# Experts' first norm moved from ScalarE to VectorE, row scaling from VectorE to GpSimd, and a quad's stages in eight slots instead of eleven

## The reference, cut to what matters

```python
def _moe(y):                       # for each row the expert idx = argmax(y @ Wg.T)
    h = relu(y @ W1[e] + b1[e])    # 128 -> 512
    return h @ W2[e] + b2[e]       # 512 -> 128
y = _layer_norm(x + _mha(x), g1, be1)
z = _layer_norm(y + _moe(y), g2, be2)    # times g2, plus be2
x = x + _layernorm(z)                    # a second norm, no weights, plus the residual
```

## Time and profile before

| what | value |
|---|---|
| median of the runs | 1222.24 us (1218.07 to 1223.42) |
| span of the profiled execution | 1168.2 us |
| its own device time | not listed apart; 54.0 us lie between its span and the median |
| PE busy over the span | 1051.2 us (90%) |
| DVE, ACT, POOL busy | 1032.2, 1008.1, 897.8 us |
| experts alone on TensorE | from about 1033 to 1138 us of the span |
| after TensorE's last matmul | about 30 us |

### The profile page before, as it was taken

How to read it: one execution, slowest core, us unless ns; L and a number is a source line. 1 busy time by engine, 2 the same in 40 slices (tenths; PEclk the granted TensorE clock), 3 DMA queues, 4 the chain that set the end, 5 groups by cost and what they waited for, 6 DMA issues and landing times. The chain is left out here.

```text
span 1168.2 us, 25817 instructions
## 1 busy us (share of the span) xinstructions
PE 1051.2 (90%) x8346; PEld 883.1 (76%) x8346; DVE 1032.2 (88%) x1971; ACT 1008.1 (86%) x2143; POOL 897.8 (77%) x648
## 2 busy tenths in 40 slices
PE   7699999899999999999999999879888877999990
PEld 3488887788878888788787887867565555999990
DVE  6999999899999999999999999998589987677773
ACT  3989999899999999999999999986589985678882
POOL 2499999799999999999899998978226666445455
PEclk9899999999999999999999999999899998999995
DMA  7634333243334333334334233343376656886640
GB/s 198 195 110 119 99 120 104 98 124 94 120 97 120 122 102 117 114 100 125 99 121 126 92 106 96 109 145 105 79 172 168 163 141 194 271 245 236 230 160 27
DMA packets 151746, 156.57 MB, mean 134 GB/s; under 512 B 47136, under 2 KB 97058, under 8 KB 151614
## 3 DMA queue, kind: packets, MB, share of 16 engines
q1 hardware_dynamic: 146270, 142.30, 41.3%
q0 software_dynamic: 5344, 12.63, 3.0%
HBM read 111.42 MB, written 23.20 MB: 115 GB/s over the span
## 5 line engine op out<-in xcount | busy, mean ns | idle before, releaser
L1169 POOL TENSOR_TENSOR cm<-rows_or_blocks 128x1024 f32<-128x1024 f32 x256 | 604.0, 2371 | 77.5 <-DVE rows_or_blocks L982 75.9
L982 DVE TENSOR_TENSOR_SCAN rows_or_blocks<-abuf,hstate,bank_pair 128x512 f32<-128x512 f32 x512 | 612.2, 1260 | 16.2 <-PE bank_pair L511 6.1
L534 PE MATMUL bank_pair<-ident,cm 128*128 128x128 f32 x2048 | 252.6, 273 | 1.2 <-POOL cm L1169 1.2
L534 PEld LDWEIGHTS bank_pair<-ident,cm 128*128 128x128 f32 x2048 | 229.7, 141 | 10.7 <-issue 8.5
L778 ACT ACTIVATE abuf<-xg_or_delta,aneg 128x512 f32<-128x512 f32 x256 | 166.6, 712 | 4.2 <-DVE rows_or_blocks L982 3.4
L778 ACT ACTIVATE abuf<-delta,aneg 128x512 f32<-128x512 f32 x256 | 166.4, 713 | 4.3 <-DVE rows_or_blocks L982 4.3
L514 PE MATMUL bank_pair<-ident,ub 128*128 128x128 f32 x1024 | 135.2, 274 | 12.4 <-ACT ub L789 6.9
L514 PEld LDWEIGHTS bank_pair<-ident,ub 128*128 128x128 f32 x1024 | 117.0, 142 | 30.9 <-issue 20.5
L429 PE MATMUL bank_pair<-xnT,rows_or_blocks 128*128 128x512 f32 x256 | 124.2, 601 | 5.1 <-DVE xnT L955 3.1
L2446 POOL DMA_INDIRECT out<-res,tokens x71 | 73.5, 1035 | 65.9 <-DVE res L2417 45.3
L789 ACT ACTIVATE ub<-vs_or_uT,bT 128x256 f32<-128x256 f32 x256 | 108.6, 497 | 0.2
(11 more groups left out here) (300 smaller groups left out, 1957.1 us busy)
## 6 DMA issues: line engine op xcount, KB each, us to landing
rows_or_blocks<-c_rows SPq DMA_DIRECT2D x256, 256.0 KB, 3.2
w_of_tile<-w SPq DMA_DIRECT2D x71, 256.0 KB, 2.7
rows_or_blocks<-routed SPq DMA_DIRECT2D x71, 128.5 KB, 2.4
xT_and_rstd<-in_xt SPq DMA_DIRECT2D x16, 257.5 KB, 3.6
xres<-in_x SPq DMA_DIRECT2D x16, 256.0 KB, 3.9
x_rows<-x1t SPq DMA_DIRECT2D x16, 256.0 KB, 3.7
xg_or_delta<-x_rows SPq DMA_DIRECT2D x16, 256.0 KB
v_rows<-vs_or_uT SPq DMA_DIRECT2D x16, 256.0 KB
```

Of the source, the lines that this page charges most:

```text
L534: mm = pe.matmul(ps_y[j // 2][:, (j % 2 * CH + c) * P:(j % 2 * CH + c + 1) * P], cm[:, n % CM_RING, c, j * P:(j + 1) * P], ident[:, :], is ...
L982: dve.tensor_tensor_scan(hbuf[:, n % RING, c, :], abuf[:, n % RING, c, :], ps_bx[n % 2 * CH + c][:, :], hstate[:, bass.ds(g * (NST * CH) + ...
L1169: pool.tensor_tensor(cm[:, n % CM_RING, :, :], hbuf[:, n % RING, :, :], c, ALU.mult).then_inc(s_cm, 1)
```

## The change

`norm_a` on ScalarE, the shift for it, and the pair of whole-quad operations `affine` go. In their place VectorE does two three-operand operations a tile: `centre_and_weigh` (slot 7), sum less mean times g2, and `scale_and_shift` (slot 8), times the reciprocal root plus be2. `scale_rows` goes to GpSimd, in slot 3, behind the scatters of the quad three before and ahead of the next scatters; it waits until `add_rows` of the quad before is done. `stats_b` is in slot 9 (was 11), its root in 10 (was 12), its shift in 11 (was 13), `norm_b` in 11 and 12 (was 14, 15), `add_x1` and `scatter` in 13 (was 16). `zn` is gone and `rows_and_expert` has one buffer.

```diff
-    ROOT_STEPS = 3
+    ROOT_STEPS = (2, 3)
+    STATS = (3, 2)
...
-    summed = sb("rows_and_expert", [P, 2, 4, D])
-    zn = sb("zn", [P, 2, 4, D])
+    summed = sb("rows_and_expert", [P, 4, D])
...
                 else:
-                    pe.wait_ge(S["stats_a"], 4 * (q - 2))
+                    pe.wait_ge(S["stats_a"], STATS[0] * (q - 3) + 1)
...
             for half in range(2):
-                for q in due(s, 14 + half):
+                for q in due(s, 11 + half):
                     norm_b(q, half)
-                for q in due(s, 8 + half):
-                    norm_a(q, half)
             for q in due(s, 7):
-                root(0, S["stats_a"], S["roots_a"], S["zn_ready"], q)
-            for q in due(s, 12):
+                root(0, S["stats_a"], S["roots_a"], S["z_ready"], q)
+            for q in due(s, 10):
                 root(1, S["stats_b"], S["roots_b"], S["z_out_ready"], q)
...
+        def centre_and_weigh(q):
+            dve.wait_ge(S["stats_a"], STATS[0] * (q + 1))
+            for i in range(tiles_of(q)):
+                b = dve.scalar_tensor_tensor(out=zg[:, i, :], in0=summed[:, i, :], scalar=mv_a[:, i, 0:1],
+                                             in1=w["rows"][:, 4, :], op0=ALU.subtract, op1=ALU.mult)
+            b.then_inc(S["zg_ready"], 1)
+
+        def scale_and_shift(q):
+            dve.wait_ge(S["roots_a"], ROOT_STEPS[0] * (q + 1))
             dve.wait_ge(S["zg_ready"], q + 1)
             if q >= 2:
                 dve.wait_ge(S["z_out_ready"], q - 1)
-            dve.tensor_tensor(z[:, q % 2, 0:n, :], zg[:, 0:n, :], row(5, n), ALU.add).then_inc(S["z_ready"], 1)
+            for i in range(tiles_of(q)):
+                b = dve.scalar_tensor_tensor(out=z[:, q % 2, i, :], in0=zg[:, i, :], scalar=rstd[0][:, i:i + 1],
+                                             in1=w["rows"][:, 5, :], op0=ALU.mult, op1=ALU.add)
+            b.then_inc(S["z_ready"], 1)
...
         def slot(s):
...
+            for q in due(s, 11):
+                less_mean(q)
             for q in due(s, 13):
-                less_mean(1, S["roots_b"], S["z_out_ready"], q)
+                add_x1(q)
             for q in due(s, 8):
-                less_mean(0, S["roots_a"], S["zn_ready"], q)
+                scale_and_shift(q)
             for q in due(s, 6):
                 add_rows(q)
                 stats_a(q)
-            for q in due(s, 5):
-                scale_rows(q)
-            for q in due(s, 16):
-                add_x1(q)
-            for q in due(s, 10):
-                affine(q)
-            for q in due(s, 11):
+            for q in due(s, 7):
+                centre_and_weigh(q)
+            for q in due(s, 9):
                 stats_b(q)
...
+        def scale_rows(q):
+            n = tiles_of(q)
+            if q == 0:
+                for i in range(4):
+                    pool.wait_ge(S[f"w1_loaded{i}"], 32)
+            else:
+                pool.wait_ge(s_rows[q % 4], 16 * sum(tiles_of(r) for r in range(q % 4 or 4, q + 1, 4)))
+                pool.wait_ge(S["stats_a"], STATS[0] * (q - 1) + 1)
+            pool.tensor_tensor(scaled[:, 0:n, :], rows[:, q % RINGS, 0:n, 0:D],
+                               w["rows"][:, 2, :].unsqueeze(1).broadcast_to([P, n, D]), ALU.mult)\
+                .then_inc(S["rows_scaled"], 1)
+
         def slot(s):
-            for q in due(s, 16):
+            for q in due(s, 3):
+                scale_rows(q)
+            for q in due(s, 13):
                 scatter(q)
```

More of the change, by code:

```diff
@@ L2132, in experts @@
     rstd = [sb(f"d_rstd_{c}", [P, 4]) for c in "ab"]
-    shift = [sb(f"d_shift_{c}", [P, 4]) for c in "ab"]
+    shift = sb("d_shift_b", [P, 4])
     names = """w1_loaded0 w1_loaded1 w1_loaded2 w1_loaded3 y_transposed yT_copied hidden_summed
-        hidden_ready expert_summed eps_set stats_a stats_b roots_a roots_b zn_ready zg_ready z_ready z_out_ready
+        hidden_ready expert_summed eps_set rows_scaled stats_a stats_b roots_a roots_b zg_ready z_ready z_out_ready
         res_ready out_scattered0 out_scattered1"""
@@ L2305, in root @@
             act.activation(rstd[n][:, :], (mv_a, mv_b)[n][:, :, 1], ACT.Ln, bias=eps[:, 0:1]).then_inc(s_out, 1)
-            act.wait_ge(s_out, ROOT_STEPS * q + 1)
+            act.wait_ge(s_out, ROOT_STEPS[n] * q + 1)
             act.activation(rstd[n][:, :], rstd[n][:, :], ACT.Exp, scale=-0.5).then_inc(s_out, 1)
-        def norm_a(q, half):
-            if half == 0:
-                act.wait_ge(S["roots_a"], ROOT_STEPS * (q + 1))
-                if q >= 2:
-                    act.wait_ge(S["zg_ready"], q - 1)
-            for i in range(2 * half, min(2 * half + 2, tiles_of(q))):
-                a = act.activation(zn[:, q % 2, i, :], summed[:, q % 2, i, :], ACT.Identity,
-                                   bias=shift[0][:, i:i + 1], scale=rstd[0][:, i:i + 1])
-            if half == 1:
-                a.then_inc(S["zn_ready"], 1)
         def norm_b(q, half):
             if half == 0:
-                act.wait_ge(S["roots_b"], ROOT_STEPS * (q + 1))
+                act.wait_ge(S["roots_b"], ROOT_STEPS[1] * (q + 1))
                 if q >= 2:
@@ L2326, in norm_b @@
                 a = act.activation(z_out[:, q % 2, i, :], z[:, q % 2, i, :], ACT.Identity,
-                                   bias=shift[1][:, i:i + 1], scale=rstd[1][:, i:i + 1])
+                                   bias=shift[:, i:i + 1], scale=rstd[1][:, i:i + 1])
             if half == 1:
@@ L2355, in stats @@
             if q >= 1:
-                dve.wait_ge(s_used, ROOT_STEPS * q)
+                dve.wait_ge(s_out, ROOT_STEPS[n] * q)
             for i in range(tiles_of(q)):
@@ L2359, in stats, with less_mean @@
             b.then_inc(s_bn, 1)
-        def less_mean(n, s_out, s_used, q):
-            dve.wait_ge(s_out, ROOT_STEPS * q + 2)
+        def less_mean(q):
+            dve.wait_ge(S["roots_b"], ROOT_STEPS[1] * q + 2)
             if q >= 1:
-                dve.wait_ge(s_used, q)
-            dve.scalar_tensor_tensor(out=shift[n][:, :], in0=(mv_a, mv_b)[n][:, :, 0], scalar=-1.0, in1=rstd[n][:, :],
-                                     op0=ALU.mult, op1=ALU.mult).then_inc(s_out, 1)
-        def scale_rows(q):
-            n = tiles_of(q)
-            if q == 0:
-                for i in range(4):
-                    dve.wait_ge(S[f"w1_loaded{i}"], 32)
-            else:
-                dve.wait_ge(s_rows[q % 4], 16 * sum(tiles_of(r) for r in range(q % 4 or 4, q + 1, 4)))
-                dve.wait_ge(S["stats_a"], 4 * q)
-            dve.tensor_tensor(scaled[:, 0:n, :], rows[:, q % RINGS, 0:n, 0:D],
-                              w["rows"][:, 2, :].unsqueeze(1).broadcast_to([P, n, D]), ALU.mult)\
-               .then_inc(S["stats_a"], 1)
+                dve.wait_ge(S["z_out_ready"], q)
+            dve.scalar_tensor_tensor(out=shift[:, :], in0=mv_b[:, :, 0], scalar=-1.0, in1=rstd[1][:, :],
+                                     op0=ALU.mult, op1=ALU.mult).then_inc(S["roots_b"], 1)
         def add_rows(q):
@@ L2382, in add_rows @@
             dve.wait_ge(S["expert_summed"], 4 * q + n)
-            dve.wait_ge(S["stats_a"], 4 * q + 1)
-            if q >= 2:
-                dve.wait_ge(S["zn_ready"], q - 1)
-            dve.tensor_tensor(summed[:, q % 2, 0:n, :], ps_f[q % 3][:, 0:n * D].rearrange("p (i d) -> p i d", i=n),
+            dve.wait_ge(S["rows_scaled"], q + 1)
+            dve.tensor_tensor(summed[:, 0:n, :], ps_f[q % 3][:, 0:n * D].rearrange("p (i d) -> p i d", i=n),
                               scaled[:, 0:n, :], ALU.add).then_inc(S["stats_a"], 1)
         def stats_a(q):
-            dve.wait_ge(S["stats_a"], 4 * q + 2)
-            stats(lambda i: summed[:, q % 2, i, :], stat_a, mv_a, S["stats_a"], 4 * q + 2, S["roots_a"], q)
-        def row(i, n):
-            return w["rows"][:, i, :].unsqueeze(1).broadcast_to([P, n, D])
-        def affine(q):
-            n = tiles_of(q)
-            dve.wait_ge(S["zn_ready"], q + 1)
-            if q >= 1:
-                dve.wait_ge(S["z_ready"], q)
-            dve.tensor_tensor(zg[:, 0:n, :], zn[:, q % 2, 0:n, :], row(4, n), ALU.mult).then_inc(S["zg_ready"], 1)
+            dve.wait_ge(S["stats_a"], STATS[0] * q + 1)
+            stats(lambda i: summed[:, i, :], stat_a, mv_a, S["stats_a"], STATS[0] * q + 1, S["roots_a"], 0, q)
+        def centre_and_weigh(q):
[6 more added lines that the diff above has]
+            dve.wait_ge(S["roots_a"], ROOT_STEPS[0] * (q + 1))
             dve.wait_ge(S["zg_ready"], q + 1)
```

6 lines of the change are left out of this document (3 added, 3 removed).

## The result

The changed kernel takes **1229.08 us** (median of 5 runs, 1227.20 to 1233.27); beside it the kernel before took 1218.07 (5 runs, 1215.90 to 1223.42). Ratio 1.0084, 95% interval 1.0057 to 1.0110: slower by 7 to 13 us. Forecast were 1218.1 us and a chance of 0.07 for slower. The forecast is wrong, and the time lies outside the range.

A forecast was written before the change was run, and what follows sets the result against it. TensorE was taken to bound the steady experts, and the delay to quad 15's result plus GpSimd's scatters the tail. Terms: 0 steady, -4.85 tail, +0.75 padding, together -4.1 us from 1222.24 to 1218.1 us; range 1213.5 to 1222.

The forecast's parts named there:

- My sum is made against the profiled span of 1168.2 us: Whole kernel: savings and costs were summed on one profile's 1168.2 us span, then put on the median of 1222.24 us.
- outside the span 54 us up to the median; both stay: Whole kernel: 54 us outside the span, and 8 us between the last scatter's issue and the span's end, stay unchanged.
- Cost in the steady stretch: 0.: Experts alone, 1033 to 1138 us: TensorE's 8.02 us a quad covers VectorE's new work and waits, so 0 us.
- ScalarE's relu and copy keep about 1 us in hand: Experts' steady stretch: ScalarE's relu and copy have about 1 us to spare before they would delay TensorE.
- Group 15 ... 13 us in hand, cost 0.: Attention's tail: group 15 scattered at about 1030.6 instead of 1021.8 us, wanted at 1043.74, so cost 0.
- padi ... +0.75 us.: Attention's tail: VectorE's padi comes at 1019.57 instead of 1018.82 us and delays TensorE through SyncE's queue by 0.75 us.
- The tail: 4.85 us earlier.: After TensorE's end: quad 15's scatters start 5.5 us earlier, and GpSimd's last scatter issue comes 4.85 us earlier.
- The pause behind them: Tail: GpSimd stands still for 1.1 us between quad 15's scatters and quad 16's, whose residual comes later.
- The new operations' price: VectorE's three-operand operations take 1.04 to 1.13 us for four, bounds 0.87 and 1.37; eight a quad.
- The rival with VectorE's period: Steady stretch: at 0.6 us per new operation VectorE's period becomes the bound, 1231 us; chance 0.06 including a combined case.
- VectorE and GpSimd stop each other: Experts: GpSimd's multiplication and VectorE's two-input SBUF operations exclude each other, tail 1.2 us later, 1219.3 us; chance 0.15.
- No row of this trace shows the case: Earlier trace: no row was said to show VectorE's two-input SBUF operation and GpSimd's operation excluding each other.

The follow-up runs named there:

- e14: Changed kernel with experts' and attention's routing scatters in pairs, and quad 1's two pairs moved to slots 20 and 21: 1179.18 us, ratio 0.9635.
- e6: Kernel before with one scatter a slot (16 to 19), each behind a further expert sum, still four in a row: 1227.3 us, ratio 1.0033.
- e7: Changed kernel with the experts' scatters one to a slot (13 to 16), so that they come in pairs: 1199.3 us, ratio 0.9804.
- e9: Kernel before with each quad's four experts' scatters in two pairs, the second two slots later: 1200.0 us, ratio 0.9787.
- e1: Kernel before, unchanged, timed and profiled again: 1224.0 us, ratio 0.9997, profiled span 1223.6 us.
- e13: Changed kernel with the four scatters of the experts' quad 1 moved to slot 20, behind the scaling for quad 4: 1227.5 us, ratio 1.0047.
- e2: Changed kernel with only the row scaling moved back from GpSimd to VectorE, in slot 5: 1233.3 us, ratio 1.0088.
- e12: Changed kernel with experts' and routing scatters in pairs, and quad 0's pairs moved to slots 16 and 17: 1181.5 us, ratio 0.9673.
- e10: Changed kernel with the experts' scatters in pairs and attention's routing scatters in two pairs too (slots 21 and 23): 1181.5 us, ratio 0.9660.

## Why the prediction was wrong, step by step

- **"My sum is made against the profiled span of 1168.2 us"; "outside the span 54 us up to the median; both stay."** This failed first. The 54 us lie inside it, and for the most part they were ScalarE's gaps and what they cost, in attention and in the experts: the changed kernel with its scatters in pairs runs 43.9 us under the kernel before (e14). A profile 4% shorter than every run of its kernel is of another course of events, and the rest of its rows tell of that one.
- **"Cost in the steady stretch: 0."** Measured: +6.0 us (1.7 to 8.5 over all profiles). The step that failed is "ScalarE's relu and copy keep about 1 us in hand", and that this covers everything. 1.3 us are in hand, but the relu comes 2.5 and 3.35 us late in the two quads shown, in a gap beside GpSimd's scatters that the prediction had no term for. The loss goes with the new slots; by what path is open, since the place of the scatters doesn't explain e6. Where the gaps are gone (e7 against e9) the step is right: 72.7 us both.
- **"Group 15 ... 13 us in hand, cost 0."** The delay came (6.5 us against e1; 8.8 forecast). Its cost did not come by the path that was looked at, SyncE's row loads, but by GpSimd's own queue: the delayed scatters joined the next four, and ScalarE stood still for 5.85 us and TensorE for 4.34. +5.4 us between tiles 16 and 28 (+5.7 from 12 on), of which 3.0 are back with the row broken (e13), most of them as faster busy time; 2.7 are open.
- **"padi ... +0.75 us."** Not to be seen; tile 16 starts 1.5 us earlier than in e1, no more than attention's own gaps vary.
- **"The tail: 4.85 us earlier."** Right, path and size: from the last outward group to the span's end 25.0 against 30.3, 5.3 us; 5.4 in e7 against e9. Quad 15's scatters start 3.5 us behind it and not 8.6: 5.1 us earlier (5.5 forecast). The pause behind them was 0.40 us and not 1.1.
- **The new operations' price**: four in 1.14 us (1138.43), forecast 1.04 to 1.13, bounds 0.87 and 1.37; in three groups 2.74 to 2.84 and in one 1.42, where GpSimd's multiplication runs beside them. GpSimd's multiplication 1.19, forecast 1.28.
- **The rival with VectorE's period** did not happen; it had the right sign and the wrong mechanism. Neither it nor any other rival asked what GpSimd's scatters do to another engine.
- **The rival "VectorE and GpSimd stop each other"** exists. It makes three groups of four in the changed kernel 1.6 to 1.7 us longer, and one 0.3, but e2, where it can't happen, is no faster. "No row of this trace shows the case" was a miss: the trace of the kernel before has it twice, in a small operation. It is told below.

## What to carry to other kernels

Hold a profile's span against the median of the runs before reading it: here 2 us lie around a span, and the gap of 54 meant that the profile showed another kind of execution, and the missing time is the first thing to find. When stages are moved, follow GpSimd's DMA queue by itself, and count how many indirect transfers it issues back to back: pairs with a pause cost nothing here, four in a row 1 to 2 us of TensorE in most quads (none in one execution), eight over 4. Take two profiles of a kernel before a difference of a few us in one stretch is given a cause. Moving stages to other slots cost more here than the work that was moved; the path of that cost is open.

## What the runs showed of the hardware

**ScalarE and SyncE stall during a row of GpSimd's indirect scatters.** The gap begins some 2 us behind the first of four (1135.95 and 1138.30 above) and lasts 1.5 to 4.4 us, 5.9 us and then 2.4 with eight and 8.1 and 4.1 with twelve. With pairs it is gone between tiles 28 and 64 in e7, e9 and e12; e10 has one gap there and e14 four, of 1.5 to 1.9 us, which cost TensorE 0.5 us in all. ScalarE records no instruction, and the matmuls that its next relu needs have long ended. VectorE and GpSimd go on. SyncE's four padding writes took 5.65 us (1055.71), beside 2.05 in the earlier trace rows and 1.93 in e13 (1056.18), where the row is broken. Not only its DMA issues are slow: a register operation between these writes took 0.68 us (1056.43) and 0.04 in e13 (1056.04). What ScalarE lacks there is open. The traces hold no record of it, and the execution of the earlier trace rows had the same rows of scatters without it. It wasn't tried whether fewer rows a scatter, or another target, would lift it.

**A three-operand operation of VectorE waits for GpSimd's multiplication.** In e7 the scaling falls onto the second shift. Timelines of VectorE and GpSimd, e7:

```profile
1127.71 1.14 DVE L2352 SCALAR_TENSOR_TENSOR d_shift_b<-d_mv_b,d_rstd_b 128x4 f32<-128x4 f32 x1
1128.78 1.13 DVE L2369 SCALAR_TENSOR_TENSOR zg<-rows_and_expert,d_mv_a,row_params 128x128 f32<-128x128 f32 x4
...
1127.62 1.20 POOL L2434 TENSOR_TENSOR rows_scaled<-rows_or_blocks,row_params 128x512 f32<-128x512 f32 x1
```

The shift on 128x4 takes 0.13 us where GpSimd multiplies nothing beside it (the changed kernel, 1138.31), and 1.14 here, ending with GpSimd's operation at 1128.82. So it is in all 12 places of e7 where it begins beside that operation, 1.10 us in the mean, and TensorE's 8.1 us a quad hide it. In the changed kernel the gaps have mostly moved the scaling to where VectorE waits anyway; four times it falls onto the new operations, and a group of four takes 2.74 to 2.84 us in place of 1.14 (1047.45, 1085.81, 1183.38), or 1.42 (1203.03). The bn_stats and bn_aggr beside it keep their time. The Trainium skill (SBUF — State Buffer, the section on its two separate sides) says that a VectorE operation with two SBUF inputs and a GpSimd operation that reads SBUF lock each other out for a whole instruction; these rows agree. The trace of the kernel before shows it too, where attention's shift begins 0.71 us behind GpSimd's multiplication and ends with it; that shift takes 0.13 to 0.16 us in 28 of its 30 places:

```profile
844.21 1.28 POOL L2066 TENSOR_TENSOR xb<-xn_or_u,row_params 128x512 f32<-128x512 f32 x1 [5.80 <-ACT xn_or_u L1643]
...
844.92 0.59 DVE L1754 SCALAR_TENSOR_TENSOR b_shift<-b_mv,b_rstd 128x4 f32<-128x4 f32 x1
```
